# A recurrent layer in 128 dependent steps: input products cut at any matmul, three more joint candidates, states added to x four at a time

## The chip, the cores and the metric

The kernel runs on one core of a Trainium2 chip. The metric is the device time of one execution in microseconds, here the median of 3 runs. TensorE (PE in the profile) multiplies, VectorE (DVE) and ScalarE (ACT) work on its results, SyncE (SP) issues the transfers, GpSimd (POOL) does almost nothing.

## What is computed

A gated recurrent layer over 128 steps, with 512 inputs, 512 hidden values and a batch of 64; its states are added to its input. All is fp32. Cut to what matters:

```python
def step(h, inp):
    x_t, prop = inp                        # prop: (t + 1) % 4 == 0 and t < 127
    comb = concatenate([x_t, h])
    z = sigmoid(comb @ Wz + bz)
    r = sigmoid(comb @ Wr + br)
    h_cand = tanh(concatenate([x_t, r * h]) @ Wh + bh)
    h_new = (1.0 - z) * h + z * h_cand
    h_next = where(prop, tanh(h_new @ Wp + bp), h_new)
    return (h_next, h_new)
return x + scan(step, h0, x)               # of h_new, over 128 steps
```

## The kernel before

**Two kinds of work.** The input products `x @ W` don't depend on the state; the recurrent products `h @ W` do, and a step can't begin before the one ahead of it has made `h`. The kernel puts input products of the next block between the recurrent products of a step, so that TensorE has work while VectorE and ScalarE make the next operand. A block is 8 steps; below, place s of a block is `t % 8`.

**Numbers in two halves.** Each fp32 operand is a sum of two fp16 values, hi and lo, and a product is lo x hi + hi x hi + hi x lo. For a recurrent product, `rec` (L1341) issues 16 matmuls of 64 columns for each of the three. Where a gate is *joint*, `rec_both` (L1350) issues 16 matmuls of 128 columns for the two that share the weights `wrec_hi`. Their results lie in two halves of a PSUM bank, which VectorE must add (`TENSOR_REDUCE`: L1037 for the reset gate R, L1055 for the update gate Z, L1072 for the candidate C), ahead of ScalarE's sigmoid or tanh (L585). Where it is not joint, ScalarE reads the bank itself (L591). `JOINT` is the range of steps in which Z is joint, R is so at the places `JOINT_RESET_AT = (0, 1, 2, 4, 5, 6)`, C at `JOINT_CANDIDATE_AT`.

**Input products.** For blocks 2 to 14 (`SEVEN`) a 2 x 2 scheme with seven products in place of eight is used: 21 *stages* a block, (gate, product) in the list `ORDER`, each of 12 matmuls of 256 columns (L1260). In block m the stages of block m + 1 are issued. `STAGES_AT` tells how many whole stages each step has. At a joint reset 4 of their matmuls (`AHEAD_OF_C`) go between Z and C, and at a joint candidate 4 more (`WITHIN_C`) inside C; the rest follows C and covers the time in which the next `h` is made. At places 3 and 7 there is one more product of the chain, PROP, with stages ahead of it and behind it.

**Who empties the banks.** A finished stage is read by ScalarE, product 1 with one `COPY` (L564), products 2, 3, 4 and 7 with two `ACTIVATE`s (L551, `begin_quarter`), or by VectorE, products 5 and 6 with one op (L963, `end_quarter`). ScalarE's order in a step is: sigmoid R, splits of x, sigmoid Z, tanh C, the bias and input for R and Z of the next step (seeds, L613 or L622), the reads of finished stages, the seed for C. Then comes sigmoid R of the next step.

**VectorE's order in a step:** add R's halves (L1037), q = r * h as hi (L1042), full and lo, add Z's halves (L1055), splits of x for a later block (`split_slot`, L890, at `SLOT_AT`), add C's halves (L1072), keep (L1076), new (L1096), the new h as hi (L1105), full (L1108) and lo (L1026), then h added to x (L1113), the scale of x at place 0 (L849 to L854), sums of x (L950), `end_quarter`. All engines run their list in order: what is late is late for all that stands behind it.

Of the kernel before, what the change touches and what calls it, by code (L numbers as in the profile page):

```python
# [69 lines left out]
def gru_kernel(nc, x, h0, wz, wr, wh, wp, biases, out):  # L70
# [109 lines left out]
    with ExitStack() as ctx:  # L180
# [207 lines left out]
        def begun(t, n, stages):  # L388

            if n != stages[0] or not joint_reset(t):  # L390
                return 0
            return AHEAD_OF_C + (WITHIN_C if joint_candidate(t) else 0)
# [106 lines left out]
        def _(act):  # L499
# [202 lines left out]
            for t in range(T):  # L702
                m, s = divmod(t, BLOCK)
                first, middle, last = (n // PER_GROUP for n in fill_of(t))
                stages_first, stages_last = stages_of(t)
# [790 lines left out]
```

## Time and profile before

| | |
|---|---|
| median of 3 runs | 1042.9 us (1042.11 to 1043.37) |
| the profiled execution: time, span | 1043.28 us, 1041.3 us |
| busy of the span: PE, PEld, DVE, ACT | 99%, 92%, 85%, 75% |
| granted TensorE clock | 1.00 |
| matmuls recorded | 20826 |
| DMA | 47.27 MB, 45 GB/s in the mean |

The span runs from the first to the last instruction; the 2 us around it belong to no engine. Matmuls overlap, and their recorded durations contain the way through the array: the time that one costs is the distance to the start of the next. The timeline puts matmuls of one kind in a run together (x16) if nothing stands between them. Block 7 (t = 56 to 63) begins at 490.48 us, and its places 1 to 7 at 497.24, 505.25, 511.99, 521.48, 529.49, 536.23 and 544.24 us.

### The profile page before, as it was taken

How to read it: one execution, taken by the hardware profiler on the slowest of the kernel's cores; microseconds unless marked ns; L12 is line 12 of the kernel's file. 1: busy time of each engine (PE TensorE's matmuls, PEld its weight loads, DVE VectorE, ACT ScalarE, POOL GpSimd, SP SyncE). 2: the span in 40 equal slices, each digit the busy share in tenths (PEclk: the TensorE clock that was granted, in tenths of full speed). 3: DMA queues.
4: the chain of work that ended last, by engine and by line, in shares of the span. 5: the costliest groups of instructions: out<-in, count | busy, mean ns of one | idle time of the engine just before them, and what ended most of it. 6: DMA issues, size and time to landing. Idle time of an engine off the chain costs nothing.

```text
span 1041.3 us, 48291 instructions
## 1 busy us (share of the span) xinstructions
PE 1034.5 (99%) x20826; PEld 953.8 (92%) x20826; DVE 882.1 (85%) x2929; ACT 776.1 (75%) x1789; POOL 0.2 (0%) x4
## 2 busy tenths in 40 slices
PE   9999999999999999999999999999999999999998
PEld 4578999999999999999999999999999999999998
DVE  6978888898888998888988888988889988776665
ACT  5877777787777777777777777877777777665565
POOL 0000000000000000000000000000000000000000
PEclk9999999999999999999999999999999999999999
DMA  9312211001111001111011110011110000000001
GB/s 326 114 62 66 83 54 43 31 15 43 43 43 43 22 25 43 43 43 42 5 42 43 43 43 23 23 43 43 43 43 17 30 23 23 23 24 24 24 4 44
DMA packets 38485, 47.27 MB, mean 45 GB/s; under 512 B 2176, under 2 KB 34048, under 8 KB 37888
## 3 DMA queue, kind: packets, MB, share of 16 engines
q1 hardware_dynamic: 38000, 44.12, 12.6%
q8 instruction: 164, 2.69, 1.1%
q14 instruction: 49, 0.40, 0.1%
q10 hardware_dynamic: 272, 0.07, 0.0%
HBM read 27.40 MB, written 16.78 MB: 42 GB/s over the span
## 4 chain that ended last, share of the span: by engine, by line
PE 96%; DVE 2%; DMA 1%; SPq 0%; issue 0%; ACT 0%; DVEq 0%
PE acc L1346 37%; PE x_acc L1260 33%; PE acc L1354 16%; PE x_acc L1150 8%; DMA x_part<-wz_dram 1%; PE x_acc L1281 0%; ACT gate L585 0%; DVE x_lo L890 0%; DVE gate L1037 0%; DVE gate L1055 0%; DVE q_split L1026 0%; DVE q_split L1042 0%; DVE h_split L1105 0%; SPq L415 0%; SPq L412 0%
## 5 line engine op out<-in xcount | busy, mean ns | idle before, releaser
L1260 PE MATMUL x_acc<-x_hi,win_hi 128*128 128x256 f16 x1092 | 297.7, 273 | 0.0
L1260 PE MATMUL x_acc<-x_lo,win_hi 128*128 128x256 f16 x1092 | 297.7, 273 | 0.0
L1260 PE MATMUL x_acc<-x_hi,win_lo 128*128 128x256 f16 x1092 | 297.6, 273 | 0.0
L585 ACT ACTIVATE gate<-gate,unscale 128x128 f32<-128x128 f32 (+1 forms) x303 | 124.2, 434 | 129.0 <-DVE gate L1055 80.5
L591 ACT ACTIVATE gate<-acc,unscale 128x128 f32<-128x128 f32 (+1 forms) x397 | 127.6, 370 | 95.3 <-PE acc L1346 93.5
L1346 PE MATMUL acc<-h_split,wrec_lo 128*128 128x64 f16 x4096 | 180.2, 193 | 0.4 <-DVE h_split L1105 0.4
L1354 PE MATMUL acc<-h_split,wrec_hi 128*128 128x128 f16 x2608 | 172.3, 219 | 0.2 <-DVE h_split L1026 0.2
L551 ACT ACTIVATE x_part<-x_acc,bias,part_unscale 128x256 f32<-128x256 f32 x312 | 154.6, 560 | 17.8 <-PE x_acc L1260 17.7
L1346 PE MATMUL acc<-q_split,wrec_hi 128*128 128x64 f16 x3968 | 160.2, 193 | 0.0
L1346 PEld LDWEIGHTS acc<-h_split,wrec_lo 128*128 128x128 f16 x4096 | 155.0, 98 | 5.5 <-issue 0.6
L1354 PEld LDWEIGHTS acc<-h_split,wrec_hi 128*128 128x128 f16 x2608 | 148.2, 98 | 0.3 <-DVE h_split L1026 0.3
L1346 PEld LDWEIGHTS acc<-q_split,wrec_hi 128*128 128x128 f16 x3968 | 135.1, 98 | 0.0
L613 ACT ACTIVATE acc<-x_part,half_seed_scale 128x512 f32<-128x512 f32 x198 | 130.6, 685 | 0.0
L1346 PE MATMUL acc<-h_split,wrec_hi 128*128 128x64 f16 x2976 | 126.4, 193 | 0.0
L1346 PE MATMUL acc<-q_split,wrec_lo 128*128 128x64 f16 x2544 | 120.5, 193 | 0.4 <-DVE q_split L1042 0.4
L1260 PEld LDWEIGHTS x_acc<-x_hi,win_lo 128*128 128x128 f16 x1092 | 106.8, 98 | 11.2
L1260 PEld LDWEIGHTS x_acc<-x_hi,win_hi 128*128 128x128 f16 x1092 | 106.8, 98 | 10.6
L1260 PEld LDWEIGHTS x_acc<-x_lo,win_hi 128*128 128x128 f16 x1092 | 106.8, 98 | 10.1
L1346 PEld LDWEIGHTS acc<-q_split,wrec_lo 128*128 128x128 f16 x2544 | 98.5, 98 | 6.2 <-issue 1.1
L1346 PEld LDWEIGHTS acc<-h_split,wrec_hi 128*128 128x128 f16 x2976 | 103.5, 98 | 0.0
L622 ACT ACTIVATE acc<-x_part,seed_scale 128x256 f32<-128x256 f32 x185 | 85.5, 477 | 1.8
L1096 DVE SCALAR_TENSOR_TENSOR new<-gate,scale 128x128 f32<-128x128 f32 x254 | 77.5, 348 | 0.9 <-ACT gate L591 0.9
(147 smaller groups left out, 1508.3 us busy)
## 6 DMA issues: line engine op xcount, KB each, us to landing
out_dram<-x_blk SPq DMA_DIRECT2D x30, 512.0 KB, 3.2
x_blk<-x_dram SPq DMA_DIRECT2D x24, 512.0 KB, 3.8
x_blk<-x_dram SPq DMA_DIRECT2D x3, 1024.0 KB, 9.2
x_part<-wz_dram SPq DMA_DIRECT2D x4, 256.0 KB, 7.2
x_part<-wh_dram SPq DMA_DIRECT2D x4, 256.0 KB, 7.0
x_part<-wr_dram SPq DMA_DIRECT2D x1, 1024.0 KB, 11.4
x_part<-wz_dram SPq DMA_DIRECT2D x1, 1024.0 KB, 13.6
x_part<-wh_dram SPq DMA_DIRECT2D x1, 1024.0 KB, 17.3
```

The lines of the kernel that those rows point to most:

```text
L551: nc.scalar.activation(part_quarter(m, g, jh, nh)[:, j], in_halves(x_acc[bank][:])[:, j], ACT.Identity, bias=bias[:, g, 2 * jh + j:2 * jh ...
L585: nc.scalar.activation(gate[g][:, half], gate[g][:, half], func, scale=unscale[:, g:g + 1]).then_inc(gate_ready[g], 1)
L591: nc.scalar.activation(gate[g][:, half, :], acc[g][:, half, :], func, scale=unscale[:, g:g + 1]).then_inc(gate_ready[g], 1)
L613: nc.scalar.activation(acc_bank[g][:], added.unsqueeze(1).broadcast_to([P, 2, KC, B]), ACT.Copy, scale=half_seed_scale[:, g:g + 1]).then_i ...
L622: nc.scalar.activation(acc[g], added, ACT.Copy, scale=seed_scale[:, g:g + 1]).then_inc(seed_ready[g], 1)
L1096: nc.vector.scalar_tensor_tensor(out=new[:, half, :], in0=gate[C][:, half, :], scalar=h_scale, in1=gate[Z][:, half, :], op0=ALU.mult, op1= ...
L1150: return nc.tensor.matmul(x_acc[bank][:, 0:cols], weights[g][:, 2 * (j // 2) + k // 2, k % 2, j % 2 * P:(j % 2 + 1) * P], values[m % 2][:, ...
L1260: mm = nc.tensor.matmul(in_halves(x_acc[bank][:])[:, j], weights[g][:, slot_w, k, j * P:(j + 1) * P], in_halves(values[m % 2][:, slot_x, : ...
L1346: mm = nc.tensor.matmul(bank[:, j, :], weights[g][:, k, j * P:(j + 1) * P], values[:, k, lo, :], start=False, stop=False, skip_group_check ...
L1354: mm = nc.tensor.matmul(acc_bank[g][:, :, j, :], wrec_hi[g][:, k, j * P:(j + 1) * P], values[:, k], start=False, stop=False, skip_group_ch ...
```

## The change

- `JOINT_CANDIDATE_AT` has six places (0, 1, 3, 4, 5, 6) in place of three (1, 4, 6), and `JOINT` begins at step 19, no longer at 16.
- `ORDER` has the stages in another order, and `SHARES_AT` gives each step a number of matmuls in place of whole stages: 31, 31, 24, 24 + 14, 32, 31, 30, 23 + 12, where `STAGES_AT` had 24, 36, 24, 24 + 12, 36, 24, 36, 24 + 12. A stage is read in the step in which its last matmul is issued.
- The split of T1 (`SLOT_AT_LATER`) goes from place 2 to place 3, where that of T2 is.
- States are kept in a ring of 8 (`h_ring`), and added to x in one op of 1024 elements at places 0 and 4, in place of one of 256 elements in each step. The last four steps are added one by one.
- In a step that finishes product 1 of gate Z with other stages, its copy comes last among the reads (`in_order_of_reads`).

```diff
-JOINT = range(16, 109)
-JOINT_CANDIDATE_AT = (1, 4, 6)
+JOINT = range(19, 109)
+JOINT_CANDIDATE_AT = (0, 1, 3, 4, 5, 6)
...
-ORDER = [(0, 1), (0, 2), (0, 3), (0, 4), (0, 5), (0, 6), (1, 1), (0, 7), (1, 2), (1, 3), (1, 4), (1, 5), (1, 6),
-         (2, 1), (2, 2), (1, 7), (2, 3), (2, 5), (2, 4), (2, 6), (2, 7)]
-
-STAGES_AT = [((), (0, 1)), ((), (2, 3, 4)), ((), (5, 6)), ((7, 8), (9,)), ((), (10, 11, 12)), ((), (13, 14)), ((), (15, 16, 17)), ((18, 19), (20,))]
+ORDER = [(0, 1), (0, 2), (1, 1), (0, 3), (0, 4), (0, 5), (0, 6), (1, 3), (0, 7), (1, 2), (1, 4), (1, 5), (1, 6),
+         (2, 1), (2, 2), (1, 7), (2, 3), (2, 4), (2, 5), (2, 6), (2, 7)]
+
+SHARES_AT = [(0, 31), (0, 31), (0, 24), (24, 14), (0, 32), (0, 31), (0, 30), (23, 12)]
 
 SLOT_AT = {2: (5, 6, 6, 8, 8, 9, 10), 3: (4, 5, 6, 7, 7, 8, 9)}
-SLOT_AT_LATER = (1, 2, 3, 4, 5, 6, 7)
+SLOT_AT_LATER = (1, 3, 3, 4, 5, 6, 7)
...
-        return STAGES_AT[s] if m + 1 in SEVEN else ((), ())
+        if m + 1 not in SEVEN:
+            return 0, 0, 0
+        first = sum(map(sum, SHARES_AT[:s]))
+        return first, first + SHARES_AT[s][0], first + sum(SHARES_AT[s])
+
+    def finished(begin, end):
+
+        return range(begin // PER_GROUP, end // PER_GROUP)
+
+    def in_order_of_reads(stages):
+
+        return sorted(stages, key=lambda n: ORDER[n] == (Z, 1))
...
-        h_even_odd = [sb("h_even", [P, KC, B]), sb("h_odd", [P, KC, B])]
+        h_ring = sb("h_ring", [P, KC, BLOCK, B])
...
+        def results_at(t):
+
+            if t >= T - CHUNK:
+                return [range(t - CHUNK, t), range(t, t + 1)] if t % CHUNK == 0 else [range(t, t + 1)]
+            return [range(t - CHUNK, t)] if t and t % CHUNK == 0 else []
...
                 else:
                     for n in range(first, last):
                         copy_group(n)
                         seed_behind(n, late, t + 1)
-                    for n in stages_last:
+                    for n in in_order_of_reads(finished(stages_middle, stages_last)):
                         read_stage(m + 1, n)
...
-                nc.vector.scalar_tensor_tensor(out=x_blk[m % RING][:, :, s, :], in0=h_out[:], scalar=h_unscale,
-                                               in1=x_blk[m % RING][:, :, s, :], op0=ALU.mult, op1=ALU.add).then_inc(out_ready, 1)
+                for steps in results_at(t):
+                    results = x_blk[steps.start // BLOCK % RING][:, :, steps.start % BLOCK:steps.start % BLOCK + len(steps)]
+                    states = h_ring[:, :, steps.start % BLOCK:steps.start % BLOCK + len(steps)]
+                    if steps[-1] == t:
+                        dve.wait_ge(h_new_ready, 2 * t + 2)
+                    nc.vector.scalar_tensor_tensor(out=results, in0=states, scalar=h_unscale, in1=results, op0=ALU.mult,
+                                                   op1=ALU.add).then_inc(out_ready, len(steps))
...
-            def stage(m, n, begin=0, stop=PER_GROUP):
-
-                g, product = ORDER[n]
-                slot_w, slot_x = FACTORS[product]
-                bank = bank_of(g, product)
-                if begin == 0:
-                    wait_stage(m, n)
-                for i in range(begin, stop):
+            def stages(m, first, last):
+
+                for at in range(first, last):
+                    n, i = divmod(at, PER_GROUP)
+                    g, product = ORDER[n]
+                    slot_w, slot_x = FACTORS[product]
+                    bank = bank_of(g, product)
+                    if i == 0:
...
-                    stage(m + 1, (stages_first + stages_last)[0], AHEAD_OF_C, AHEAD_OF_C + WITHIN_C)
+                    stages(m + 1, stages_first + ahead_of_candidate(t), stages_first + begun(t))
...
-                for n in stages_last:
-                    stage(m + 1, n, begun(t, n, stages_first + stages_last))
+                    stages(m + 1, stages_first + begun(t), stages_last)
...
-    nc = bacc.Bacc("TRN2", target_bir_lowering=False, num_devices=1)
+    nc = bacc.Bacc("TRN2", target_bir_lowering=False, num_devices=1, dynamic_dma_scratch_size=8192)
```

How instructions move, at three places. First VectorE from the end of place 4 (lo of the new h) to place 5, in block 7. Before:

```order
L1026 TENSOR_TENSOR h_split<-h_even,h_split 128x2x64 x2
L1113 SCALAR_TENSOR_TENSOR x_blk3<-h_even,unscale,x_blk3 128x4x64
L963 SCALAR_TENSOR_TENSOR x_part0<-x_acc2,part_unscale,x_part0 128x2x256
L963 SCALAR_TENSOR_TENSOR x_part0<-x_acc3,part_unscale,x_part0 128x2x256
L1037 TENSOR_REDUCE gate0<-acc0 128x128 x2
```

With the change:

```order
L1045 TENSOR_TENSOR h_split<-h_ring,h_split 128x2x64 x2
L1137 SCALAR_TENSOR_TENSOR x_blk3<-h_ring,unscale,x_blk3 128x4x256
L982 SCALAR_TENSOR_TENSOR x_part0<-x_acc2,part_unscale,x_part0 128x2x256
L982 SCALAR_TENSOR_TENSOR x_part0<-x_acc3,part_unscale,x_part0 128x2x256
L1056 TENSOR_REDUCE gate0<-acc0 128x128 x2
```

The op that adds states to x has become one of 4 x 256 elements and stands, as before, ahead of the two `end_quarter`s and of R's addition for place 5. The same op stands ahead of the scale of x at the end of place 0.

Second, VectorE at place 3, from lo of q to the new state as hi. Before:

```order
L1026 TENSOR_TENSOR q_split<-q_full,q_split 128x2x64 x2
L1055 TENSOR_REDUCE gate1<-acc1 128x256
L890 SCALAR_TENSOR_TENSOR x_lo1<-sum_b,x_scale,x_hi1 128x512
L1076 SCALAR_TENSOR_TENSOR keep<-gate1,h_even 128x256
L1096 SCALAR_TENSOR_TENSOR new<-gate2,scale,gate1 128x128 x2
L1105 TENSOR_TENSOR q_split<-new,keep 128x2x64 x2
```

With the change:

```order
L1045 TENSOR_TENSOR q_split<-q_full,q_split 128x2x64 x2
L1074 TENSOR_REDUCE gate1<-acc1 128x256
L909 SCALAR_TENSOR_TENSOR x_lo1<-sum_a,x_scale,x_hi1 128x512
L909 SCALAR_TENSOR_TENSOR x_lo1<-sum_b,x_scale,x_hi1 128x512
L1091 TENSOR_REDUCE gate2<-acc2 128x128 x2
L1095 SCALAR_TENSOR_TENSOR keep<-gate1,h_ring 128x256
L1115 SCALAR_TENSOR_TENSOR new<-gate2,scale,gate1 128x128 x2
L1124 TENSOR_TENSOR q_split<-new,keep 128x2x64 x2
```

A second split of x and the two additions of C's halves have come in ahead of the new state, on which PROP waits.

Third, ScalarE from tanh C of place 6 to sigmoid R of place 7. Before:

```order
L585 ACTIVATE gate2<-gate2,unscale 128x128 x2
L622 ACTIVATE acc0<-x_part1,seed_scale 128x256
L613 ACTIVATE acc1<-x_part1,half_seed_scale 128x512
L551 ACTIVATE x_part0<-x_acc3,bias,part_unscale 128x256 x2
L551 ACTIVATE x_part0<-x_acc0,bias,part_unscale 128x256 x2
L622 ACTIVATE acc2<-x_part1,seed_scale 128x256
L591 ACTIVATE gate0<-acc0,unscale 128x128 x2
```

With the change:

```order
L604 ACTIVATE gate2<-gate2,unscale 128x128 x2
L641 ACTIVATE acc0<-x_part1,seed_scale 128x256
L632 ACTIVATE acc1<-x_part1,half_seed_scale 128x512
L570 ACTIVATE x_part0<-x_acc3,bias,part_unscale 128x256 x2
L570 ACTIVATE x_part0<-x_acc0,bias,part_unscale 128x256 x2
L570 ACTIVATE x_part0<-x_acc1,bias,part_unscale 128x256 x2
L641 ACTIVATE acc2<-x_part1,seed_scale 128x256
L610 ACTIVATE gate0<-acc0,unscale 128x128 x2
```

The stage (2, 4) is now finished at place 6, and its two reads stand ahead of place 7's sigmoid. In the same way the copy of (1, 1) has gone from place 2 to place 1, where it stands behind two stages' reads and ahead of place 2's sigmoid.

## Rows read from the trace of the kernel before

**Rows 1.** The page: busy time of PE, its share, and matmuls.

```profile
PE 1034.5 (99%) x20826; PEld 953.8 (92%) x20826; DVE 882.1 (85%) x2929; ACT 776.1 (75%) x1789; POOL 0.2 (0%) x4
```

**Rows 2.** Waits of PE from 175 to 195 us: total, times, longest.

```profile
PE acc L1346 <- DVE q_split L1042: 0.4, 1, 0.4
```

**Rows 3.** Timeline of PE, places 1 and 2: start us, us, operation.

```profile
500.40 0.63 PE L1346 MATMUL acc<-q_split,wrec_lo 128*128 128x64 f16 x16
...
501.30 1.06 PE L1354 MATMUL acc<-q_split,wrec_hi 128*128 128x128 f16 x16
502.19 0.27 PE L1260 MATMUL x_acc<-x_hi,win_lo 128*128 128x256 f16 x1
...
505.25 0.86 PE L1346 MATMUL acc<-h_split,wrec_lo 128*128 128x64 f16 x24
505.95 1.06 PE L1354 MATMUL acc<-h_split,wrec_hi 128*128 128x128 f16 x16
```

**Rows 4.** Timeline of PE: C of place 2, PROP of place 3, C of place 5.

```profile
508.41 0.40 PE L1346 MATMUL acc<-q_split,wrec_lo 128*128 128x64 f16 x8
...
518.77 0.40 PE L1346 MATMUL acc<-q_split,wrec_lo 128*128 128x64 f16 x8
...
532.65 0.40 PE L1346 MATMUL acc<-q_split,wrec_lo 128*128 128x64 f16 x8
```

**Rows 5.** Timeline of DVE at 190 us (t = 18).

```profile
190.42 0.75 DVE L1037 TENSOR_REDUCE gate<-acc 128x128 f32<-128x256 f32 x2
191.31 0.63 DVE L1042 TENSOR_TENSOR q_split<-gate,h_odd 128x128 f16<-128x128 f32 x2
```

**Rows 6.** Timeline of PE at the same place, with idle time before and its releaser.

```profile
191.12 0.27 PE L1260 MATMUL x_acc<-x_hi,win_hi 128*128 128x256 f16 x1
191.75 0.39 PE L1346 MATMUL acc<-q_split,wrec_lo 128*128 128x64 f16 x8 [0.35 <-DVE q_split L1042]
```

**Rows 7.** Timeline of DVE, place 1.

```profile
499.03 0.76 DVE L1037 TENSOR_REDUCE gate<-acc 128x128 f32<-128x256 f32 x2
...
502.54 0.75 DVE L1072 TENSOR_REDUCE gate<-acc 128x128 f32<-128x256 f32 x2
503.20 0.42 DVE L1076 SCALAR_TENSOR_TENSOR keep<-gate,h_even 128x256 f32<-128x256 f32 x1
```

**Rows 8.** Timeline of DVE, place 3.

```profile
516.10 0.75 DVE L890 SCALAR_TENSOR_TENSOR x_lo<-sum_b,x_scale,x_hi 128x512 f16<-128x512 f32 x1
516.76 0.42 DVE L1076 SCALAR_TENSOR_TENSOR keep<-gate,h_even 128x256 f32<-128x256 f32 x1
...
517.63 0.48 DVE L1105 TENSOR_TENSOR q_split<-new,keep 128x128 f16<-128x128 f32 x2
```

**Rows 9.** Timeline of DVE, end of place 4 and beginning of place 5.

```profile
529.50 0.49 DVE L1113 SCALAR_TENSOR_TENSOR x_blk<-h_even,unscale,x_blk 128x256 f32<-128x256 f32 x1
529.90 1.41 DVE L963 SCALAR_TENSOR_TENSOR x_part<-x_acc,part_unscale,x_part 128x512 f32<-128x512 f32 x2
531.28 0.76 DVE L1037 TENSOR_REDUCE gate<-acc 128x128 f32<-128x256 f32 x2
```

**Rows 10.** Timeline of ACT, place 1 to the sigmoid of place 2; a copy.

```profile
504.86 1.91 ACT L551 ACTIVATE x_part<-x_acc,bias,part_unscale 128x256 f32<-128x256 f32 x4
506.66 0.48 ACT L622 ACTIVATE acc<-x_part,seed_scale 128x256 f32<-128x256 f32 x1
507.50 0.73 ACT L585 ACTIVATE gate<-gate,unscale 128x128 f32<-128x128 f32 x2 [0.37 <-DVE gate L1037]
...
512.19 0.57 ACT L564 COPY x_acc<-x_acc 128x512 f32<-128x512 f32 x1 [0.19 <-PE x_acc L1260]
```

**Rows 11.** Timeline of ACT, end of place 6 to the sigmoid of place 7.

```profile
545.43 0.48 ACT L622 ACTIVATE acc<-x_part,seed_scale 128x256 f32<-128x256 f32 x1
546.07 0.63 ACT L591 ACTIVATE gate<-acc,unscale 128x128 f32<-128x128 f32 x2 [0.17 <-PE acc L1346]
```

**Rows 12.** One line's instructions (L861 of DVE): count, durations, form.

```profile
L861 DVE SCALAR_TENSOR_TENSOR win_lo<-x_part,scale,win_hi x2: 1276/1281/1286, 23.9 to 25.2; 128x1024 f16<-128x1024 f32 x2
```

More of the change, by code:

```diff
@@ L386, in candidates_before, with ahead_of_candidate, begun @@
             return sum(joint_candidate(step) for step in range(t))
[L388 to L392, printed above, removed]
+        def ahead_of_candidate(t):
+            return AHEAD_OF_C if joint_reset(t) else 0
+        def begun(t):
+            return ahead_of_candidate(t) + (WITHIN_C if joint_candidate(t) else 0)
+        def results_at(t):
+            if t >= T - CHUNK:
+                return [range(t - CHUNK, t), range(t, t + 1)] if t % CHUNK == 0 else [range(t, t + 1)]
+            return [range(t - CHUNK, t)] if t and t % CHUNK == 0 else []
         def props_before(t):
@@ L761, in _ @@
                         seed_behind(n, late, t + 1)
-                    for n in stages_first:
+                    for n in finished(stages_first, stages_middle):
                         read_stage(m + 1, n)
@@ L768, in _ @@
                         seed_behind(n, late, t + 1)
-                    for n in stages_last:
+                    for n in finished(stages_middle, stages_last):
                         read_stage(m + 1, n)
@@ L1030, in _ @@
                 props = props_before(t)
-                h_in = h_prop if t % CHUNK == 0 else h_even_odd[(t - 1) % 2]
-                h_out = h_even_odd[t % 2]
+                h_in = h_prop[:] if t % CHUNK == 0 else h_ring[:, :, (t - 1) % BLOCK]
+                h_out = h_ring[:, :, t % BLOCK]
                 if joint_reset(t):
@@ L1075, in _ @@
                 dve.wait_ge(gate_ready[Z], t + 1)
-                nc.vector.scalar_tensor_tensor(out=keep[:], in0=gate[Z][:], scalar=-1.0, in1=h_in[:], op0=ALU.add,
+                nc.vector.scalar_tensor_tensor(out=keep[:], in0=gate[Z][:], scalar=-1.0, in1=h_in, op0=ALU.add,
                                                op1=ALU.mult).then_inc(keep_ready, 1)
@@ L1125, in _ @@
                         split_x(m + 2, k)
-                for n in stages_of(t)[0] + stages_of(t)[1]:
+                stages_first, _, stages_last = stages_of(t)
+                for n in finished(stages_first, stages_last):
                     if ORDER[n][1] in (5, 6):
@@ L1362, in _ @@
                 first, middle, last = fill_of(t)
-                stages_first, stages_last = stages_of(t)
+                stages_first, stages_middle, stages_last = stages_of(t)
                 if t == 0:
@@ L1398, in _ @@
                     if joint_reset(t):
-                        stage(m + 1, (stages_first + stages_last)[0], stop=AHEAD_OF_C)
+                        stages(m + 1, stages_first, stages_first + AHEAD_OF_C)
                 else:
@@ L1447, in _ @@
                     fill(first, middle)
-                    for n in stages_first:
-                        stage(m + 1, n, begun(t, n, stages_first))
+                    stages(m + 1, stages_first + begun(t), stages_middle)
                     if props == 0:
@@ L1466, in _ @@
                     fill(middle, last)
+                    stages(m + 1, stages_middle, stages_last)
                 else:
                     fill(first, last)
-                for n in stages_last:
-                    stage(m + 1, n, begun(t, n, stages_first + stages_last))
+                    stages(m + 1, stages_first + begun(t), stages_last)
 def kernel(x, cond_1024, L0_cond_Wz, L0_cond_bz, L0_cond_Wr, L0_cond_br, L0_cond_Wh, L0_cond_bh, L0_cond_Wp, L0_cond_bp):
```

9 lines of the change are left out of this document (5 added, 4 removed).

## Prediction

> **What bounds the kernel now.** I read the page first: PE is busy 99% of the span [rows 1]. Recorded matmuls overlap, so this alone says little; the timeline of PE tells whether it issues without a hole. It does. In block 7 sixteen matmuls of 128 columns take 0.89 us (501.30 to 502.19), 28 of 256 take 3.06 (to 505.25), 24 of 64 take 0.70 (to 505.95) [rows 3]: 0.056, 0.109 and 0.029 each, and wherever I looked in the joint blocks one follows the other at that distance. The Trainium skill (Trainium Kernel Development and Optimization, Performance Expectations) calls matmul busy time a bad metric and weight loads busy a good one; PEld is busy 92%, by which TensorE would have 80 us to spare. The distances between starts say that it has almost nothing, and they decide.
>
> So TensorE's list is the bound, and VectorE and ScalarE are hidden, but narrowly. Where VectorE was late in this trace, PE waited: at t = 18 R's halves are added from 190.42, q's hi starts at 191.31 [rows 5], and C begins at 191.75 where 191.23 would have followed the stage ahead of it [rows 6]. The list of waits names this one [rows 2]; with two more at t = 16 it comes to 1.5 us by the distances. Two prices follow: from the start of R's addition to C's first matmul at least 1.33 us, from the start of a hi op on VectorE to the matmul that reads it 0.44.
>
> The slack left elsewhere, as rows: place 1 adds R from 499.03 [rows 7] and C begins at 500.40 [rows 3]: 1.37, slack 0.04. Place 5: 531.28 [rows 9] to 532.65 [rows 4], again 0.04, and VectorE came free only 0.06 before. Place 3: PROP's hi starts at 517.63 [rows 8], PROP at 518.77 [rows 4]: slack 0.70. Place 2: ScalarE is free at 506.66 + 0.40 = 507.06 and begins its sigmoid at 507.50 [rows 10], C follows at 508.41 [rows 4]: slack 0.44 + 0.03. Place 7: free at 545.83, sigmoid at 546.07 [rows 11]: slack 0.24, and some 0.1 behind it.
>
> **The change on TensorE's list.** A joint candidate puts 16 matmuls of 128 columns (0.89) in place of 32 of 64 (32 x 0.0292 = 0.93): it saves 0.04. Places and range give 68 joint candidates in place of 35, 33 x 0.04 = 1.4 us. JOINT from 19 makes Z and R plain at t = 16, 17, 18: six times 0.04 back, 0.2. The stages' 252 matmuls a block stay, only moved. Sum: -1.2 us. The three waits at t = 16 to 18 should go too, since without reductions VectorE has about 1.3 us less in each of these steps: -1.5.
>
> **The change on VectorE and ScalarE.** The start-to-start prices: a split of 512 elements 0.66 (516.10 to 516.76) [rows 8], C's two halves 0.66 (502.54 to 503.20) [rows 7], h added to x 0.40 (529.50 to 529.90) [rows 9]. The wide addition isn't in the trace; an op of the same kind over 1024 elements lasts 1.28 [rows 12], less 0.09 by which the next one overlaps (0.49 against 0.40 for the narrow one): 1.19. It can't be under 0.40 or over 1.60, four narrow ones. I take 1.19, since kind and size are the same. Per block it saves VectorE 2 x (1.60 - 1.19) = 0.8 us, but all of it lands in two steps, +0.79 in each. ScalarE's reads: four in 1.80 (504.86 to 506.66), a copy 0.57 less 0.11 of overlap, 0.46 [rows 10].
>
> Joint C takes TensorE from C's start to its end 1.79 with the 4 stages inside (500.40 to 502.19) [rows 3] in place of 48 x 0.0292 = 1.40: +0.39, paid for by 4 fewer behind. Now place by place, later engine against earlier TensorE:
>
> - A, place 1's C. Place 0 ends with the wide addition, +0.79, and has C's halves new, +0.66. TensorE's place 0 is +0.39 and 23 stage matmuls behind C in place of 20, +0.33. Late by 0.79 + 0.66 - 0.72 - 0.04 = 0.69; some hundredths of idle in VectorE's place 0 may take up a part. I take 0.65.
> - B, place 2's C. The copy of (1, 1) now stands ahead of the sigmoid, +0.46; TensorE comes 5 stage matmuls sooner (23 for 28), 0.55, and ScalarE's slack was 0.47; place 1's chain is 0.04 tighter: 0.58 late.
> - C, PROP of place 3. The second split +0.66, C's halves +0.66; TensorE +0.39 - 4 x 0.109 = -0.05. 1.32 + 0.05 - 0.70 = 0.67 late.
> - D, place 5's C. The wide addition +0.79 ahead of two `end_quarter`s that aren't moved; TensorE 4 matmuls sooner, 0.44; slack 0.04 + 0.06: 1.13 late.
> - E, place 7's C. One more stage's two reads, +0.90; TensorE 6 matmuls sooner (22 for 28), 0.66; slack 0.24 + 0.1: 1.22 late.
>
> Each is a wait at the head of PE's queue: all that stands behind it, C, the stages and the next step, moves by as much, and the engines behind it are then on time with TensorE again, so that the next place starts with the slack it had. I find no cover: the stages behind C can't be issued ahead of it. Places 0, 4 and 6 keep 0.1 to 0.3. One block: 0.65 + 0.58 + 0.67 + 1.13 + 1.22 = 4.25 us.
>
> The Trainium skill (ScalarE: Activation LUTs, What ACT_TABLE_LOAD costs) gives an ACTIVATE with immediates 186 ns + 0.833 an element and 93 ns for each pointer operand, less 93 of overlap: for a read of 256 elements with two pointers that is 0.49 us where the row has 0.45. By it E would be 0.08 longer and the whole under 1 us longer. The row is used.
>
> Blocks 3 to 12 have all five: 42.5. Block 2 (joint from place 3) has C, D, E: 3.0. Block 13 has no split and no sum for a later block: B at 0.4, and D at about 1.2, where the scale of x for the last block stands too, 1.6 in all. Blocks 0, 1, 14 and 15 are plain: VectorE has idle time there, and I cost them at nothing; if the wide addition at place 4 of block 1 isn't covered it is 0.3. Moving stores by up to three steps costs nothing: a slot of the ring for x is loaded again four blocks before its use. Sum: 42.5 + 3.0 + 1.6 - 1.2 - 1.5 = +44.4. The profiled execution would go from 1043.3 to 1087.7, the median, 0.4 under it, from 1042.9 to 1087.
>
> **Rivals.**
> - *As the two edited lists may be meant: TensorE never waits.* Then only its list counts: 1042.9 - 1.2 - 1.5 = 1040.2, faster. For it: stages were cut to single matmuls, so that each gap can be filled exactly, and TensorE had no hole before. Against: at D the arithmetic misses by 1.1 us, with 0.1 of slack in the rows. It decides if VectorE at the end of place 4 has 1.1 us less to do than its rows say, for which the wide addition would have to be almost free. Chance 0.06.
> - *Only VectorE's three places wait,* because ScalarE's reads have room that I don't see: 10 x (0.65 + 0.67 + 1.13) + 1.8 + 1.2 - 2.7 = +25, 1068. For it: B and E hang on ScalarE's order, where a wait for a stage can hide other work. Against: no idle time stands ahead of these reads in rows 10 and 11. Chance 0.15.
> - *Lateness is carried on:* after a late C the next h has 0.1 to 0.2 of slack, PROP's tanh at place 3 stands behind four reads, and lo halves are needed within 0.1. If each block loses 1 to 2 us more: 1098 to 1108. Chance 0.13.
> - *No measurable change,* if waits and gains cancel: nothing here is of a size with it. Chance 0.02.
> - My forecast: 0.64, in 1078 to 1096 by itself (each of five terms by 0.1 to 0.2, ten times).
>
> **Numbers.** The time is the likeliest case's, 1087. The range has to reach the second rival and most of the third: 1064 to 1101, with the first rival, the fourth and the end of the third outside. A measurement of this kernel tells 0.2% from nothing, 2.1 us: faster 0.06, same 0.02, slower 0.92.
>
> **What would show it.** In the list of waits of PE: acc <- q_split behind VectorE's q hi, about 10 times each at places 1, 2, 5 and 7, and q_split <- new, keep ahead of PROP at place 3; a block of 8 steps in 67 us, where it took 63; idle time in PE's timeline in front of C at place 5 of 1.1 us; VectorE with idle time at places 2 and 7 behind ScalarE's gate. Blocks 14 and 15 as long as before. The addition of 1024 elements at 1.28 us. If it were 0.5, A and D go and 1068 or less follows. If place 7's sigmoid doesn't stand directly behind six reads, E is wrong. If waits at t = 16 to 18 are still there, the 1.5 is.

## The result, and the profile after

| | median | runs |
|---|---|---|
| before | 1042.51 us | 4, 1042.0 to 1043.37 |
| with the change | 1098.97 us | 4, 1098.83 to 1099.09 |

The ratio is 1.0542, with a 95% interval of 1.0529 to 1.0555: slower by 56 us, where 44 had been forecast. The span of the profiled execution went from 1041.3 to 1097.2 us, the granted clock is 1.00 in both.

The page of the changed kernel, beside [rows 1]: the span, each engine's busy time, and the chain that ended last by engine.

```profile
span 1097.2 us, 47418 instructions
...
PE 1046.8 (95%) x20394; PEld 952.4 (87%) x20394; DVE 885.5 (81%) x2893; ACT 784.0 (71%) x1789; POOL 0.2 (0%) x4
...
PE 50%; DVE 30%; ACT 14%; issue 4%; DMA 2%; SPq 1%; DVEq 0%; ACTq 0%
```

TensorE's share fell from 99% to 95%. That understates what was lost, since recorded matmuls overlap: one of 256 columns is recorded with 0.27 us and the next starts 0.109 behind it. The chain tells more: TensorE had 96% of it before and has 50% now; the rest runs over VectorE, ScalarE and issuing.

The waits of PE in the whole span (total us, times, longest), beside [rows 2]:

```profile
PE acc L1372 <- DVE q_split L1061: 37.8, 48, 1.8
PE acc L1372 <- DVE q_split L1124: 5.3, 11, 0.5
PE x_acc L1286 <- DVE x_part L982: 2.0, 11, 0.4
```

That view leaves short waits out, and of each it counts only the time behind the last matmul's recorded end. From here on a wait is the distance between the starts of two matmuls less the distance of its kind (0.029, 0.056, 0.109 or 0.216 us for 64, 128, 256, 512 columns). Counted so behind the first 40 us, the waits went from 2.5 to 59.6 us, +57.1; all the matmuls of the kernel at their distances come to 1023.5 us before and 1022.4 after, -1.1. The two changes together, +56.0, are the change of the span.

Block 7 begins at 515.46 and ends at 583.65, 68.2 us, where it had 63.3. The first matmul behind each of its longer waits, beside [rows 3, 4], with the idle time ahead of it and its releaser: C of places 1 and 2, PROP of place 3, C of 5 and 7, a stage of place 7. (At place 5 this block is the odd one: it waits 1.33 us by the distances, the other blocks 1.14.)

```profile
526.71 0.47 PE L1372 MATMUL acc<-q_split,wrec_lo 128*128 128x64 f16 x10 [0.44 <-DVE q_split L1061]
...
534.94 0.39 PE L1372 MATMUL acc<-q_split,wrec_lo 128*128 128x64 f16 x8 [0.58 <-DVE q_split L1061]
...
545.91 0.39 PE L1372 MATMUL acc<-q_split,wrec_lo 128*128 128x64 f16 x8 [0.48 <-DVE q_split L1124]
...
561.03 0.65 PE L1372 MATMUL acc<-q_split,wrec_lo 128*128 128x64 f16 x16 [1.16 <-DVE q_split L1061]
...
576.69 0.39 PE L1372 MATMUL acc<-q_split,wrec_lo 128*128 128x64 f16 x8 [1.06 <-DVE q_split L1061]
...
582.33 0.28 PE L1286 MATMUL x_acc<-x_hi,win_hi 128*128 128x256 f16 x1 [0.16 <-DVE x_part L982]
```

VectorE at places 0 and 1, beside [rows 7, 12]; at place 3, beside [rows 8]; at places 4 and 5, beside [rows 9]:

```profile
523.43 1.28 DVE L1137 SCALAR_TENSOR_TENSOR x_blk<-h_ring,unscale,x_blk 128x1024 f32<-128x1024 f32 x1
...
525.39 0.75 DVE L1056 TENSOR_REDUCE gate<-acc 128x128 f32<-128x256 f32 x2
526.28 0.62 DVE L1061 TENSOR_TENSOR q_split<-gate,h_ring 128x128 f16<-128x128 f32 x2
...
542.63 0.74 DVE L909 SCALAR_TENSOR_TENSOR x_lo<-sum_a,x_scale,x_hi 128x512 f16<-128x512 f32 x1
543.29 0.74 DVE L909 SCALAR_TENSOR_TENSOR x_lo<-sum_b,x_scale,x_hi 128x512 f16<-128x512 f32 x1
543.96 0.75 DVE L1091 TENSOR_REDUCE gate<-acc 128x128 f32<-128x256 f32 x2
...
545.48 0.48 DVE L1124 TENSOR_TENSOR q_split<-new,keep 128x128 f16<-128x128 f32 x2
...
557.19 1.28 DVE L1137 SCALAR_TENSOR_TENSOR x_blk<-h_ring,unscale,x_blk 128x1024 f32<-128x1024 f32 x1
558.38 1.41 DVE L982 SCALAR_TENSOR_TENSOR x_part<-x_acc,part_unscale,x_part 128x512 f32<-128x512 f32 x2
559.70 0.75 DVE L1056 TENSOR_REDUCE gate<-acc 128x128 f32<-128x256 f32 x2
560.59 0.62 DVE L1061 TENSOR_TENSOR q_split<-gate,h_ring 128x128 f16<-128x128 f32 x2
```

The 1024-wide addition takes 1.28, and the next op starts 1.20 and 1.19 behind it (523.43 to 524.63, the first op of the scale of x; 557.19 to 558.38). C begins 1.32 and 1.33 behind the start of R's addition (525.39 to 526.71, 559.70 to 561.03), PROP 0.43 behind its hi op, as in the trace of before. The timeline marks no idle time of VectorE in any of these stretches: what C and PROP wait for there is the end of VectorE's list of work.

ScalarE at places 1 to 2 and 6 to 7, beside [rows 10, 11], and the four reads ahead of PROP's tanh between them:

```profile
531.20 1.91 ACT L570 ACTIVATE x_part<-x_acc,bias,part_unscale 128x256 f32<-128x256 f32 x4
533.19 0.57 ACT L583 COPY x_acc<-x_acc 128x512 f32<-128x512 f32 x1
533.67 0.48 ACT L641 ACTIVATE acc<-x_part,seed_scale 128x256 f32<-128x256 f32 x1
534.08 0.68 ACT L604 ACTIVATE gate<-gate,unscale 128x128 f32<-128x128 f32 x2
...
546.27 1.91 ACT L570 ACTIVATE x_part<-x_acc,bias,part_unscale 128x256 f32<-128x256 f32 x4
548.07 0.63 ACT L610 ACTIVATE gate<-acc,unscale 128x128 f32<-128x128 f32 x2
...
572.75 2.81 ACT L570 ACTIVATE x_part<-x_acc,bias,part_unscale 128x256 f32<-128x256 f32 x6
575.45 0.49 ACT L641 ACTIVATE acc<-x_part,seed_scale 128x256 f32<-128x256 f32 x1
575.84 0.64 ACT L610 ACTIVATE gate<-acc,unscale 128x128 f32<-128x128 f32 x2
```

Both sigmoids (534.08 and 575.84) stand behind their reads, with only the seed for C between, and without idle time.

### The profile page after: what moved, and what is told of

Read it like the earlier page. It is cut to its first block, busy times and chain, and to the rows that moved or that the text cites. A ratio compares the mean times of both kernels' runs of the same rounds, so it can differ in the third digit from the quotient of the medians.

```text
span 1097.2 us, 47418 instructions
## 1 busy us (share of the span) xinstructions
PE 1046.8 (95%) x20394; PEld 952.4 (87%) x20394; DVE 885.5 (81%) x2893; ACT 784.0 (71%) x1789; POOL 0.2 (0%) x4
## 4 chain that ended last, share of the span: by engine, by line
PE 50%; DVE 30%; ACT 14%; issue 4%; DMA 2%; SPq 1%; DVEq 0%; ACTq 0%
PE acc L1372 23%; PE x_acc L1286 15%; PE x_acc L1175 7%; PE acc L1380 5%; ACT x_part L570 4%; ACT gate L604 4%; DVE x_lo L909 3%; DVE x_part L982 3%; DVE gate L1074 3%; DVE q_split L1061 3%; DVE gate L1091 3%; DVE x_blk L1137 2%; DVE q_split L1045 2%; DVE gate L1056 2%; ACT acc L632 2%
## 5 line engine op out<-in xcount | busy, mean ns | idle before, releaser
L604 ACT ACTIVATE gate<-gate,unscale 128x128 f32<-128x128 f32 (+1 forms) x360 | 144.1, 428 | 159.2 <-DVE gate L1074 77.7
L610 ACT ACTIVATE gate<-acc,unscale 128x128 f32<-128x128 f32 (+1 forms) x340 | 111.1, 376 | 115.6 <-PE acc L1372 115.5
L1380 PE MATMUL acc<-h_split,wrec_hi 128*128 128x128 f16 x2512 | 166.2, 220 | 0.0
L1372 PE MATMUL acc<-q_split,wrec_lo 128*128 128x64 f16 x2544 | 115.6, 193 | 43.3 <-DVE q_split L1061 37.8
L632 ACT ACTIVATE acc<-x_part,half_seed_scale 128x512 f32<-128x512 f32 x225 | 147.6, 679 | 1.9 <-ACT x_part L570 1.9
L1372 PE MATMUL acc<-h_split,wrec_hi 128*128 128x64 f16 x3168 | 134.7, 194 | 0.0
L1372 PE MATMUL acc<-q_split,wrec_hi 128*128 128x64 f16 x2912 | 119.1, 194 | 0.0
L1061 DVE TENSOR_TENSOR q_split<-gate,h_ring 128x128 f16<-128x128 f32 x192 | 53.8, 292 | 76.3 <-ACT gate L610 60.4
L1372 PEld LDWEIGHTS acc<-q_split,wrec_hi 128*128 128x128 f16 x2912 | 100.0, 98 | 0.0
L1056 DVE TENSOR_REDUCE gate<-acc 128x128 f32<-128x256 f32 x134 | 50.5, 419 | 40.1 <-PE acc L1380 40.1
```

The source lines that it names most:

```text
L604: nc.scalar.activation(gate[g][:, half], gate[g][:, half], func, scale=unscale[:, g:g + 1]).then_inc(gate_ready[g], 1)
L610: nc.scalar.activation(gate[g][:, half, :], acc[g][:, half, :], func, scale=unscale[:, g:g + 1]).then_inc(gate_ready[g], 1)
L632: nc.scalar.activation(acc_bank[g][:], added.unsqueeze(1).broadcast_to([P, 2, KC, B]), ACT.Copy, scale=half_seed_scale[:, g:g + 1]).then_i ...
L1056: nc.vector.tensor_reduce(flat(gate[R][:, half]), acc_bank[R][:, :, half].rearrange("p n k b -> p (k b) n"), AX_X, ALU.add).then_inc(reset ...
L1061: nc.vector.tensor_tensor(q_split[:, half, 0, :], gate[R][:, half, :], h_in[:, half, :], ALU.mult).then_inc(q_hi_ready, 1)
L1372: mm = nc.tensor.matmul(bank[:, j, :], weights[g][:, k, j * P:(j + 1) * P], values[:, k, lo, :], start=False, stop=False, skip_group_check ...
```

## The experiments

Each of these kernels ran once, but for 8, 10 and 11, whose times are medians of 10 or 11 runs; they are held against the 1098.97 us of the changed kernel or against the kernel before. That ran beside them: 1043.27 (one run) beside the first four, 1042.72 (median of 14) beside the next four, 1042.66 us (median of 21) beside the last four. The four runs of the changed kernel lie within 0.3 us, and each reading below rests on waits in the trace as well as on the time.

**1. The states added one by one again.** This undoes the wide addition; the ring stays.

```diff
         def results_at(t):
-            if t >= T - CHUNK:
-                return [range(t - CHUNK, t), range(t, t + 1)] if t % CHUNK == 0 else [range(t, t + 1)]
-            return [range(t - CHUNK, t)] if t and t % CHUNK == 0 else []
+            return [range(t, t + 1)]
```

> States are added to x one step at a time again (127 ops of 256 elements), all else as changed. Theory (what counts is where VectorE's work stands in its list, not how much of it there is): the waits at C of place 1 (0.61 us) and most of that at place 5 (1.14 to 0.35) go, 6.1 + 8.9 us; the waits of blocks 0 and 1 (4.2) go for the most part, 3.4; but the narrow op now stands ahead of the two end_quarters of place 7, whose wait grows from 0.33 to 0.73, 4.4 more, and at place 2 it costs 0.1, 1.1 more. Sum about 13 less: 1086. Rival (VectorE's sum of work per block bounds these blocks): four narrow ops cost 0.4 us more than the wide one, 0.8 a block, so no faster than 1099 and up to 1107.

1084.22 us. Place 1's wait is gone, place 5 has 0.34 of 1.14 left. Stage 20 of place 7 waits longer, 0.7 to 0.9 in place of 0.33: VectorE has one more addition there, ahead of the `end_quarter`s. The other places are unchanged to 0.03 us but for single steps, and the 0.1 expected at place 2 didn't come. 14.8 us of the 56 are the wide addition's, net.

**2. T1 split at place 2 again.**

```diff
-SLOT_AT_LATER = (1, 3, 3, 4, 5, 6, 7)
+SLOT_AT_LATER = (1, 2, 3, 4, 5, 6, 7)
```

> The split of T1 goes back to place 2, all else as changed; VectorE has the same ops. Theory: the 0.65 us wait of PROP at place 3 goes in all 11 blocks that have it, and place 2 takes the split into 0.58 us of idle: 7.1 less, 1092. The two small waits at place 4 (0.13) stay. Rival (work per block counts): unchanged at 1099 within 1.

1090.66 us, 8.3 less. PROP waits no more, and place 2 waits 0.75 as in the changed kernel: the split is hidden there.

**3. The old order of stages with the new shares.** All else is the change's.

```diff
-ORDER = [(0, 1), (0, 2), (1, 1), (0, 3), (0, 4), (0, 5), (0, 6), (1, 3), (0, 7), (1, 2), (1, 4), (1, 5), (1, 6),
-         (2, 1), (2, 2), (1, 7), (2, 3), (2, 4), (2, 5), (2, 6), (2, 7)]
+ORDER = [(0, 1), (0, 2), (0, 3), (0, 4), (0, 5), (0, 6), (1, 1), (0, 7), (1, 2), (1, 3), (1, 4), (1, 5), (1, 6),
+         (2, 1), (2, 2), (1, 7), (2, 3), (2, 5), (2, 4), (2, 6), (2, 7)]
```

> ORDER as before the change, all else as changed. Theory: the copy of (1, 1) is no longer ahead of place 2's sigmoid, nor the reads of (2, 4) ahead of place 7's, and place 7 has one end_quarter in place of two. The wait at C of place 2 goes from 0.75 to about 0.1, at place 7 from 1.22 to 0.32, and that of stage 20 (0.33) goes: 6.5 + 9.9 + 3.9, about 20 less, 1079. Rival (ScalarE's reads are not what place 7 waits for, but late sums of stages): place 7 keeps its wait, and 1090 or more.

1122.81 us, a miss by 44. The expected waits did go: place 7 has 0.32 left, place 2 nothing. But stages wait for their own bank. The waits of PE in that run:

```profile
PE x_acc L1286 <- DVE x_part L982: 18.8, 13, 1.6
...
PE x_acc L1286 <- ACT x_acc L583: 13.7, 11, 1.3
PE x_acc L1286 <- ACT x_part L570: 13.7, 11, 1.3
```

With shares of 31 and 31, a stage starts in the same step in which the one ahead of it in its bank is finished, and ScalarE or VectorE reads a bank only at the end of that step. At places 0, 1 and 2 TensorE stands for 1.4 to 1.65 us. So the new shares need the first part of the new `ORDER`, with (1, 1) third, or another that parts the stages of one bank; its tail can be put back alone, as experiment 7 shows.

**4. A load ahead of a store.** SyncE issues the load of the sums for the last weights ahead of the store of the first states, no longer behind it.

```diff
+                if m == 0:
+                    load_sums_last(R)
                 store(m, FIRST)
                 if m == 0:
                     load_half(Z, 1)
-                    load_sums_last(R)
```

> On SyncE's queue the load of the last quarter of Wr's sums goes ahead of the first store of block 0 instead of behind it and behind the load that waits for that store; all else as changed. Theory: the first store waits for the wide addition at t = 4, one step later than before the change, and holds the load of the quarter up, for which VectorE waits 3.07 us in t = 5. PE's wait at C of t = 6 (1.97) goes, that at t = 5 (0.68, of VectorE's wide addition itself) stays: 2.0 less, 1097. Rival (VectorE waits for the memory or the transfer itself, not for its turn in the queue): 1099 as it is.

1096.97 us, 2.0 less: the wait of 1.97 at t = 6 is gone.

**5. The wide addition behind `end_quarter`, at places 3 and 7.** It's still one op of 1024 elements for four states, but one step earlier and behind all that its step has for VectorE except the scaling of PROP's tanh, for which VectorE has to wait there anyway.

```diff
-            return [range(t - CHUNK, t)] if t and t % CHUNK == 0 else []
+            return [range(t - CHUNK + 1, t + 1)] if t % CHUNK == CHUNK - 1 else []
...
+                # (behind the end_quarters, no longer ahead of the scale of x)
+                for steps in results_at(t):
```

> The wide addition stands at places 3 and 7, of the four states up to that step's own, behind the end_quarters and the sum of x and ahead of PROP's result, where VectorE waits for ScalarE's tanh anyway; all else as changed. Theory (position decides): the waits at C of places 1 (0.61) and 5 (1.14) go, 18.8 us in all blocks, and with them 3.5 of the 4.2 in blocks 0 and 1, since the first store is released at t = 3 again; at place 7 VectorE ends 0.8 us behind PROP's tanh, of which 0.25 reaches the next step, 3 more. Sum: 1080. Rival (a wide op costs the same wherever it stands, because VectorE's sum of work counts): 1099.

1077.79 us, 21.2 less, and 6.4 less than with single additions. The waits of places 1 and 5 are gone and so is most of those in blocks 0 and 1; a new one of 0.16 stands at place 0.

**6. The candidate joint at three places again.**

```diff
-JOINT_CANDIDATE_AT = (0, 1, 3, 4, 5, 6)
+JOINT_CANDIDATE_AT = (1, 4, 6)
```

> Joint candidates at places 1, 4 and 6 alone, as before the change; all else as changed. Theory: without C's halves on VectorE at place 0 the wait of place 1 goes (6.1), at place 3 that of PROP (7.1); TensorE's own list is 33 x 0.043 = 1.4 longer; places 2, 5 and 7 keep their waits. 1087. Rival (the six joint candidates are the whole of the loss): 1045. Second rival (they cost nothing, the adds and reads alone do): 1100.

1086.99 us, 12.0 less. Places 1, 3 and 4 wait no more; 2, 5 and 7 keep 0.75, 1.14 and 1.23.

**7. The tail of the order alone.** (2, 4) is finished at place 7 again, so that its two reads leave the way of place 7's sigmoid.

```diff
-         (2, 1), (2, 2), (1, 7), (2, 3), (2, 4), (2, 5), (2, 6), (2, 7)]
+         (2, 1), (2, 2), (1, 7), (2, 3), (2, 5), (2, 4), (2, 6), (2, 7)]
```

> Of ORDER only the stages (2, 4) and (2, 5) change places again, as they stood before; the rest as changed. Theory: place 6 loses two reads of ScalarE, so the wait at C of place 7 goes from 1.22 to 0.32, and with one end_quarter at place 7 the wait of stage 20 (0.33) goes: 9.9 + 3.9, 1085. The new waits on copies and end_quarters at places 0 to 2 that appear with the whole of the old order don't come. Rival (those new waits come from the cut at any matmul itself, whatever the order of the first stages): over 1110.

1085.58 us, 13.4 less: C of place 7 waits 0.32 in place of 1.22, and stage 20 waits no more. Some 2 us of another kind are lost in this one run, at t = 6 and behind it (the last section): without them it would be about 15.5 less.

**8. The kernel before with the joint form from step 19.**

```diff
-JOINT = range(16, 109)
+JOINT = range(19, 109)
```

> The kernel before, with JOINT from step 19 in place of 16 and nothing else. Theory: the waits at t = 17 and 18 (1.51 us) go, since VectorE has no additions of halves there, and TensorE's list is 0.2 longer: 1.3 less, 0.9988 of before. Rival (the waits only move to t = 19 and 20): same within 0.3.

1042.14 us in 11 runs, a ratio of 0.9994 (0.9985 to 1.0003): no difference that can be told. The waits of t = 17 and 18 are gone, as forecast, and others of 0.1 to 0.26 stand at seven steps from 21 to 94.

**9. Three of the faults mended together:** the additions as in 5, the order's tail as in 7, T1 as in 2.

```diff
-         (2, 1), (2, 2), (1, 7), (2, 3), (2, 4), (2, 5), (2, 6), (2, 7)]
+         (2, 1), (2, 2), (1, 7), (2, 3), (2, 5), (2, 4), (2, 6), (2, 7)]
...
-SLOT_AT_LATER = (1, 3, 3, 4, 5, 6, 7)
+SLOT_AT_LATER = (1, 2, 3, 4, 5, 6, 7)
...
-            return [range(t - CHUNK, t)] if t and t % CHUNK == 0 else []
+            return [range(t - CHUNK + 1, t + 1)] if t % CHUNK == CHUNK - 1 else []
```

> The changed kernel with the four-state adds behind the quarter's end at places 3 and 7 (as in e5), (2, 5) back ahead of (2, 4) in the order (as in e7) and T1's share back to place 2 (as in e2). If the waits are separate prices that add: 1077.8 from e5, less 8.3 of T1, less 13.4 of the order's tail, so 1056 us, with waits of TensorE left of 0.75 us at place 2, 0.33 at place 7 and 0.13 at place 4 in a block. Rival: the waits partly hide each other, so that a mended one comes back at the next place: then 1062 us or more, with a wait of 0.3 us or more at a place that had none in e5, e2 and e7.

1053.78 us, 2 less than the sum. Those 2 us are what experiment 7 lost at t = 6 and behind it: its wait of 2.48 there, 0.5 longer than the changed kernel's, and 1.6 at the lower clock. Here, with the additions as in 5, t = 6 doesn't wait. The only wait over 0.3 us that none of experiments 2, 5 and 7 has is one of 0.53 at t = 112; one of 0.76 at t = 113 stands in 5 too. The waits of PE from 170 to 900 us have come down to one row:

```profile
PE acc L1372 <- DVE q_split L1061: 7.9, 22, 0.6
```

By the distances it is 0.74 at place 2 and 0.32 at place 7 in each block, and 0.11 at place 4.

**10. And the candidate at four other places.** Experiment 9 with one line more.

```diff
-JOINT_CANDIDATE_AT = (0, 1, 3, 4, 5, 6)
+JOINT_CANDIDATE_AT = (0, 3, 4, 5)
```

> e9 with the candidate joint at places 0, 3, 4 and 5 alone, so that the sigmoid at places 2 and 7 follows reads of half the candidate less. Theory: place 2's wait falls from 0.75 to 0.1 us (11 blocks, 7 us), place 7's from 0.32 to nothing (3.5 us), two more separate candidates a block cost 22 x 0.043 = 0.9 us of stream: 1056 - 10.5 + 0.9 = 1046 us, by 3 to 4 us slower than the kernel before. Rival: place 2's wait is that of the copy of (1, 1) for its bank, which the candidate's form doesn't move: 0.5 us of it or more stays and the time is 1051 or above.

1042.55 us in 10 runs, a ratio of 0.9999 (0.9990 to 1.0009). Places 2 and 7 wait no more, so the rival is out. It gave 11.2 us, 1.7 more than expected. With 3.4 us of waits left in all, new order, new shares and four joint candidates stand where the kernel before stands.

**11. The kernel before with the ring and the wide addition,** placed as in 5, and the joint form from 19. Order, whole stages, slots and candidates are the old ones; the edit is made on the changed kernel and cut here, `ORDER` and `SLOT_AT_LATER` go back too.

```diff
-JOINT_CANDIDATE_AT = (0, 1, 3, 4, 5, 6)
+JOINT_CANDIDATE_AT = (1, 4, 6)
...
-SHARES_AT = [(0, 31), (0, 31), (0, 24), (24, 14), (0, 32), (0, 31), (0, 30), (23, 12)]
+SHARES_AT = [(0, 24), (0, 36), (0, 24), (24, 12), (0, 36), (0, 24), (0, 36), (24, 12)]
...
```

> The kernel before with its own order, shares, slots and candidates, the joint form from step 19, and of the change the ring of states with the four-wide add, placed behind the quarter's end at places 3 and 7. Theory: the ring takes 0.8 us of VectorE's work a block off and the wide add lies where nobody waits for VectorE: waits as in the kernel before with the joint from 19, time 1041.5 to 1042.5 us, no difference that can be told. Rival: the 1.3 us add delays the next end of a reset by 0.2 us or more at place 0 or 4, 11 blocks each: 1045 us or above.

1041.07 us in 11 runs (1040.35 to 1042.39), a ratio of 0.9984 with an interval of 0.9976 to 0.9993. It is the fastest of all, 1.6 us under the kernel before and 0.4 under what was expected: a gain that the interval separates from nothing, though it is under the 0.2% named ahead. Experiment 8 has 1042.14 with the later start of the joint form alone. The kernel of 11 also has the change's `dynamic_dma_scratch_size=8192`, whose own worth no run tells. Behind the first 40 us TensorE waits 0.65 us in all, where the kernel before has 2.5. The page:

```profile
span 1038.5 us, 48435 instructions
...
PE 1033.6 (100%) x20938; PEld 954.4 (92%) x20938; DVE 865.8 (83%) x2825; ACT 774.0 (75%) x1789; POOL 0.2 (0%) x4
```

**12. The same with the wide addition at places 0 and 4,** as the change has it, ahead of the scale of x and the `end_quarter`s.

```diff
-            return [range(t - CHUNK + 1, t + 1)] if t % CHUNK == CHUNK - 1 else []
+            return [range(t - CHUNK, t)] if t and t % CHUNK == 0 else []
```

> e11 with the four-wide add where the change has it, at places 0 and 4, ahead of the work of the next step. Theory: the add's place, not its width, is the price: waits of TensorE for the end of the reset of about 0.7 us at place 5 and up to 0.7 at place 1 in a block and some 4 us in blocks 0 and 1: 1053 to 1062 us. Rival: in the old order VectorE has room there (the splits of T1 are elsewhere) and the time stays within 3 us of the kernel before.

1062.46 us, 0.5 above the theory's range: the span is 22 us longer than in 11. C waits 0.73 at place 1 and 0.70 at place 5 in each block, and 5.1 us in blocks 0 and 1 (2.0 of them at t = 6). VectorE around place 1 of block 7:

```profile
507.84 1.27 DVE L1137 SCALAR_TENSOR_TENSOR x_blk<-h_ring,unscale,x_blk 128x1024 f32<-128x1024 f32 x1
509.04 0.15 DVE L868 TENSOR_REDUCE square_sum<-acc 128x1 f32<-128x4 f32 x1
...
509.80 0.75 DVE L1056 TENSOR_REDUCE gate<-acc 128x128 f32<-128x256 f32 x2
510.68 0.62 DVE L1061 TENSOR_TENSOR q_split<-gate,h_ring 128x128 f16<-128x128 f32 x2
```

TensorE there:

```profile
511.12 0.56 PE L1372 MATMUL acc<-q_split,wrec_lo 128*128 128x64 f16 x13 [0.57 <-DVE q_split L1061]
```

The old order gives no more room than the new one does: the place of the addition costs 21.4 us in the one (1062.46 against 1041.07) and 21.2 in the other (1098.97 against 1077.79).

## Why the prediction was right, and where its sizes were off

The forecast of 1087 lay 12 us under 1099, within its range of 1064 to 1101, and its mechanism is shown. The sum against the waits of the changed kernel, in us:

| term | forecast a block | measured a block | all steps, forecast | all steps, measured | undone in |
|---|---|---|---|---|---|
| A, place 1 | 0.65 | 0.61 | 6.5 | 6.1 | 1, 5, 6 |
| B, place 2 | 0.58 | 0.75 | 5.8 | 7.5 | 3, 10 |
| C, place 3 | 0.67 | 0.65 | 7.4 | 7.1 | 2, 6 |
| D, place 5 | 1.13 | 1.14 | 12.4 | 12.7 | 5 |
| E, place 7 | 1.22 | 1.22 | 13.4 | 13.4 | 7 |
| place 4, R | none | 0.13 | 0 | 1.5 | 6 |
| place 7, stage 20 | none | 0.33 | 0 | 3.9 | 7 |
| blocks 0 and 1 | | | 0 | 4.2 | 5; 4 (t = 6) |
| blocks 13 and 14 | | | 1.6 | 3.0 | |
| waits of before that go | | | -1.5 | -2.5 | 8 |
| TensorE's list | | | -1.2 | -1.1 | |
| sum | | | 44.4 | 55.8 | |

The span went up by 56.0; the rest are waits of under 0.2 us here and there.

**What held.** A, C, D and E are within 0.05 us a block. Each rests on a price from a row and a slack from two others, with the wide addition at 1.19 from [rows 12] (1.20 measured) and the two delays of [rows 5, 6]. That the waits add, each independent of the next, held too: experiments 2, 5 and 7 give 42.9 us apart and 45.2 together, and the difference is what 7 alone lost at t = 6 and behind it. TensorE's list and "the addition of 1024 elements at 1.28 us" are right.

**B was sized too small, by 0.17.** The copy of (1, 1) was costed at its 0.46 between starts [rows 10]. In the changed kernel it overwrites the bank that the two reads just ahead of it empty, those of (0, 4), and has to wait for their end, 531.20 + 1.91 = 533.11: it starts at 533.19, where the four reads' own distance of 4 x 0.45 gives 533.00. With the 0.48 to the next op it costs 0.67. This is read from the starts; no run takes the copy's wait away by itself. In experiment 10, with place 1's candidate in two plain halves, the copy still starts 0.08 behind the end of the reads (505.21 against 503.20 + 1.93), but ScalarE gets through in time, and all of B goes.

**"Blocks 0, 1, 14 and 15 are plain ... I cost them at nothing" and "moving stores by up to three steps costs nothing" failed.** They cost 4.2 us. The argument about the stores looked at the slot of the ring, and not at what stands behind the store on SyncE's queue. The first store now waits for the addition of place 4, not of place 3, and is issued at 85.56 us, where it was 75.40. Behind it stand the load of x for block 4, which waits until the store has landed (issued at 90.53), and the last quarter of Wr's sums (91.20, where it was 86.25). VectorE in the changed kernel:

```profile
95.18 0.69 DVE L938 TENSOR_TENSOR sum_c<-sum_c,sum_b 128x512 f32<-128x512 f32 x1 [3.07 <-DMA sum_c<-wr_dram]
...
96.39 0.49 DVE L1061 TENSOR_TENSOR q_split<-gate,h_ring 128x128 f16<-128x128 f32 x2
```

It stands 3.07 us for that load, with q of t = 6 queued behind. With the load ahead of the store this wait is gone (experiment 4). The rest is the wide addition itself at t = 5 and 9 to 15, in steps that had been called idle from their kind, and not from rows; experiment 5 removes all but 0.4 of it, and 12 brings 5.1 back in the old order.

**Block 13 was costed at B and D alone,** 1.6 us. It has B at 0.60 and D at 1.32, but E too, at 0.74, since the stages of block 14 are issued there as well; one of 0.2 stands in block 14.

**Two waits were missed because only C and PROP had been asked for.** At place 7 stage 20 needs the bank that the second `end_quarter` frees. With (2, 5) behind (2, 4) that op starts later on VectorE, and TensorE waits 0.33 for it. At place 4 R waits 0.13 for h, whose PROP tanh stands behind four reads (546.27, 548.07 above). The prediction named those four reads as a rival and gave them no price.

**Waits that were there before** came to 2.5 us by the distances, not 1.5: the short ones from t = 9 on weren't counted. The two that the prediction puts at t = 16 stand in the products of h at t = 17; they and that of t = 18 go with the later `JOINT`, as experiment 8 shows. Of the others only 0.2 at t = 127 and the one at t = 9 (in the row of blocks 0 and 1) are left in the changed kernel.

**The rivals.** "TensorE never waits" fell: VectorE did have that work at place 4. Nor did a mended kernel reach its 1040: experiment 10, with four joint candidates and 3.4 us of waits, is no faster than before. "Only VectorE's three places wait" fell with E and B, 21 us. "Lateness is carried on" has at most 0.13 + 0.33 us a block to its name, under the 1 to 2 that it needed, and not even the 0.13 is shown to be carried: with PROP on time (experiment 2) 0.11 of it stays. That the result lies 12 us above the forecast comes for the most part from these two waits (5.4), blocks 0 and 1 (4.2), B (1.7) and blocks 13 and 14 (1.4), less 1.0 for waits that were there before.

**What stays open.** At t = 61 D is 1.33, where the ten others of blocks 2 to 12 have 1.14, and it is so in experiments 2, 3, 4 and 7 too. The step ahead of it shows where it comes from: VectorE starts Z's addition 0.57 us behind lo of q (552.61 to 553.18), in the next block 0.41 (620.79 to 621.20), while TensorE had issued Z equally early in both. Experiments 8 and 9 have waits of 0.1 to 0.26 us at steps that have none in their neighbours. Nothing was run that tells what holds the engines there.

The Trainium skill (Trainium Kernel Development and Optimization, Performance Expectations) names the weight loads' busy share as one of two good measures. Here it fell from 92% to 87%, while the loads' time stayed (953.8 and 952.4 us): it follows the span. Taken for room, the missing 8% would be some 80 us, an estimate, where the distances show 2.5 us of waits.

## What to carry to other kernels

Where three engines run in lock step, ask of every op put in: what stands behind it in its engine's list before the next operand that TensorE waits for, and how much slack do two start times leave there? Four narrow ops joined into one wide one save VectorE 0.4 us in four steps, and cost TensorE 0.7 in the step that has to take it, unless the wide op goes behind the last thing on which somebody waits; with the op so placed the old schedule gained 1.6 us (0.6 of it perhaps by the later start of the joint form), with it at places 0 and 4 it lost 20 in the one run made. A store that is released later holds up the loads behind it in its queue, and a stage that is cut finer needs its bank earlier: both are asked for beside the engines' own times.

## What the runs showed of the hardware

TensorE's granted clock fell in the middle of a kernel once. In experiment 7 TensorE waits 2.48 us at t = 6 and has 2.12 us busy of the 4 from 92 to 96. The windows of that run (stretch, length, busy of PE, PEld, DVE, ACT and POOL, granted clock, DMA share, GB/s):

```profile
92.00:96.00 4.00, 2.12 (x73) 2.00 (x69) 1.21 (x2) 1.11 (x3) 0.00 (x0) 1.00 0.53 178
96.00:100.00 4.00, 3.56 (x56) 2.59 (x57) 4.00 (x13) 3.31 (x9) 0.00 (x0) 0.68 0.59 181
100.00:104.00 4.00, 4.00 (x66) 2.59 (x64) 1.96 (x8) 1.81 (x5) 0.00 (x0) 0.90 0.06 20
```

TensorE works again from 96.44, and from 97.40 to 100.81 the granted clock is at the lower of its two levels, 1.2 in place of 2.4 GHz. Matmuls of 512 columns start 0.43 us apart, then 0.22:

```profile
96.44 0.39 PE L1372 MATMUL acc<-q_split,wrec_lo 128*128 128x64 f16 x8 [2.31 <-DVE q_split L1061]
...
99.67 0.63 PE L1175 MATMUL x_acc<-x_hi,win_lo 128*128 128x512 f16 x1
100.09 0.63 PE L1175 MATMUL x_acc<-x_hi,win_hi 128*128 128x512 f16 x1
...
101.32 0.38 PE L1175 MATMUL x_acc<-x_lo,win_hi 128*128 128x512 f16 x1
101.53 0.38 PE L1175 MATMUL x_acc<-x_hi,win_lo 128*128 128x512 f16 x1
```

By the distances that cost 1.6 us on top of the wait. The changed kernel waits 1.97 us at the same step, with 3.01 of the 4 us busy, and its clock stays at 1.00, as it does with waits of 1.99 and 2.01 us there in experiments 3 and 12:

```profile
92.00:96.00 4.00, 3.01 (x94) 2.77 (x92) 0.93 (x3) 1.35 (x5) 0.00 (x0) 1.00 0.62 200
```

None of the changed kernel's waits in the steady blocks, 1.33 us at most, was followed by a lower clock.
